# Eight-layer kernel on one core: experts of the second layer a round later on their own bank, ranking behind their weighing; statistics of the seventh layer first in the round

## The reference, cut to what matters

```python
def _L0_ffn_ref(x, W_qkv, b_qkv, W_gate, b_gate, W_experts, b_experts):
    ...
    attn = jax.nn.softmax(attn, axis=-1)
    attn_out = jnp.einsum('bhqk,bkhd->bqhd', attn, v).reshape(B, S, D)
    gate = jax.nn.softmax(x @ W_gate + b_gate, axis=-1)
    top_g, top_i = jax.lax.top_k(gate, TOP_K)
    combine = jnp.sum(jax.nn.one_hot(top_i, E, dtype=x.dtype) * top_g[..., None], axis=2)
    expert_out = jnp.einsum('bsd,edf->bsef', x, W_experts) + b_experts
    moe_out = jnp.einsum('bsef,bse->bsf', expert_out, combine)
    return attn_out + moe_out
```

## Time and profile before

| | us |
|---|---|
| median of 3 runs | 3958.63 (3945.28 to 3960.69) |
| the profiled execution | 3959.01 |
| its span in the profile | 3956.3 |

### The profile page before, as it was taken

The page is one execution under the profiler, slowest core; times in us unless marked ns, Lnnn a source line. Parts: engine busy times, 40 slices in busy tenths (PEclk is TensorE's granted clock), DMA queues, the critical chain, the costliest instruction groups (busy, mean ns, idle before and its releaser), DMA issues.

```text
span 3956.3 us, 106820 instructions
## 1 busy us (share of the span) xinstructions
PE 3214.9 (81%) x39458; PEld 2495.8 (63%) x39458; DVE 2607.1 (66%) x7302; ACT 1752.1 (44%) x4103; POOL 1160.3 (29%) x1193
## 2 busy tenths in 40 slices
PE   6999978888886999976689957766287999999955
PEld 5888854555553666656689945555286777777744
DVE  5677746777775787874454458888423666666679
ACT  4766744555553444432233312222043665665611
POOL 2222223333332333326520024443801223222211
PEclk9999988999997777867799977786599999999966
DMA  3000010000001000011147731110163000000000
GB/s 96 8 9 8 8 24 8 7 7 7 7 7 72 18 17 17 18 15 38 36 168 254 252 111 34 35 32 9 52 217 109 14 11 12 12 11 13 7 17 25
DMA packets 165933, 180.23 MB, mean 46 GB/s; under 512 B 45824, under 2 KB 142848, under 8 KB 165120
## 3 DMA queue, kind: packets, MB, share of 16 engines
q1 hardware_dynamic: 139728, 139.20, 10.8%
q0 software_dynamic: 25600, 28.64, 2.6%
q10 hardware_dynamic: 432, 10.19, 0.6%
HBM read 65.58 MB, written 33.03 MB: 25 GB/s over the span
## 4 chain that ended last, share of the span: by engine, by line
PE 37%; issue 24%; DVE 18%; POOL 9%; DMA 5%; ACT 2%; SPq 2%; another core or an unknown queue 2%; DVEq 0%; POOLq 0%; ACTq 0%
PE ps L965 31%; PE ps L1179 4%; DMA scr_y<-acc 3%; POOL probs L943 3%; DVE mx L1934 2%; POOL arena_a L931 2%; POOL route L937 1%; POOL rstd L920 1%; POOL scr L906 1%; DVE probs L1936 1%; PE ps L1016 1%; DVE den L1947 1%; DVE xn L1844 1%; DVE mx L1923 1%
## 5 line engine op out<-in xcount | busy, mean ns | idle before, releaser
L943 POOL TENSOR_TENSOR probs<-probs,den 128x1024 f32<-128x1024 f32 x128 | 243.2, 1901 | 768.6 <-DVE den L1949 768.6
L965 PE MATMUL ps<-small,xcT 128*64 128x64 f32 (+6 forms) x2976 | 409.6, 355 | 56.1 <-DVE oT L2042 19.7
L1590 ACT ACTIVATE pT<-ps 128x512 f32<-128x512 f32 (+1 forms) x576 | 305.0, 572 | 206.7 <-PE ps L1179 203.9
L965 PE MATMUL ps<-small,oT 128*64 128x128 f32 (+1 forms) x2304 | 326.0, 292 | 28.4 <-ACT oT L1598 16.9
L1179 PE MATMUL ps<-small,probs 128*128 128x128 f32 x2176 | 323.9, 293 | 8.2 <-ACT pT L1590 4.7
L965 PEld LDWEIGHTS ps<-small,oT 128*64 128x64 f32 (+1 forms) x2304 | 279.8, 152 | 75.1 <-ACT oT L1598 24.4
L1598 ACT ACTIVATE oT<-ps 64x512 f32<-64x512 f32 x512 | 288.9, 588 | 78.5 <-PE ps L965 75.5
L1179 PEld LDWEIGHTS ps<-small,probs 128*128 128x128 f32 x2176 | 257.1, 149 | 101.6 <-issue 40.5
L920 POOL TENSOR_TENSOR rstd<-veps,neghalf 128x2 f32<-128x2 f32 (+1 forms) x192 | 147.6, 769 | 576.8 <-DVE veps L1836 382.6
L965 PE MATMUL ps<-arena_b,qT 64*64 64x64 f32 (+3 forms) x10056 | 282.7, 232 | 29.9 <-DVE probs L1920 24.6
L931 POOL DMA_DIRECT2D arena_a<-kT x416 | 216.7, 527 | 279.8 <-ACT kT L1531 263.1
(11 more groups left out here) (291 smaller groups left out, 7454.8 us busy)
## 6 DMA issues: line engine op xcount, KB each, us to landing
wbuf<-parts SPq DMA_DIRECT2D x70, 704.0 KB, 3.5
wbuf<-parts_b SPq DMA_DIRECT2D x39, 512.0 KB, 3.0
scr_y<-acc SPq DMA_DIRECT2D x109, 128.0 KB, 3.4
xcT<-in_ctxT SPq DMA_DIRECT2D x96, 128.0 KB
arena_a<-kT SPq DMA_DIRECT2D x608, 8.0 KB
xcT<-scr SPq DMA_DIRECT2D x70, 128.0 KB, 2.2
arena_a<-kT POOLq DMA_DIRECT2D x416, 8.0 KB
xn<-scr SPq DMA_DIRECT2D x39, 128.0 KB, 2.2
```

The costliest lines, as they stand in the source:

```text
L943: pool.tensor_tensor(pr, pr, rv[:, t, 0:nh].unsqueeze(2).to_broadcast([P, nh, S]), ALU.mult).then_inc(s_probs.sem, 1)
L965: return nc.tensor.matmul(o, lhsT, rhs, start=start, stop=stop, skip_group_check=True)
L1590: nc.scalar.activation(pT[:, t, 4 * j:4 * j + n, :].rearrange("p c t -> p (c t)"), bank(b, n * P), ACT.Copy).then_inc(drained[b], 1)
```

## The change

In `l0f`, C, E and Y lose their `+`: the experts of a group are multiplied, weighed and summed in the round after the one in which it is projected and ranked. They get a ring of their own, `mid_ring`, with bank 5 alone; F, G, QK and V keep bank 4 alone. H moves from before E0.0 to behind R, L from before H to behind E0.0, C from before P1 to before E0.0, Y from before S0 to the round's end. The head sums are taken with 8 products of 256 columns where there were 32 of 64. ACT copies values and sums together into `turned_o`, now `acc` and 512 columns wide (A); PE turns four blocks (R) where it turned two; DVE takes the reciprocal of one column per head (32 where there were 256), multiplies into `o_sb` and adds that to `x_sb`. DVE's update from R now counts on `s_upd`.

In `l3x`, L stands first in the round where it stood behind K3, and M behind K0 where it stood behind W1.

```diff
--- before.py
+++ after.py
@@ -106,15 +106,17 @@
...
         self.front = []
+        self.mid = []
         self.body = []
...
                 continue
-            (self.front if lag == 1 else self.body).extend([item] * uses.get(item[0], 1))
+            part = self.front if lag == 1 else self.mid if item[0] in ("C", "E", "Y") else self.body
+            part.extend([item] * uses.get(item[0], 1))

...

-        return (self.front if item in self.front else self.body).index(item)
+        return (self.front if item in self.front else self.mid if item in self.mid else self.body).index(item)

...
@@ -136,7 +138,7 @@
...
     l0f = Layer(1, "l0f", stages(
-        "F+ S1 G+ QK+ D1 L++ H+ T0- E0.0+ T1- P0 E0.1+ A- V+ E1.0+ E1.1+ R- C+ P1 M++ Y+ S0+ D0+"),
+        "F+ S1 G+ D1 QK+ T0- C E0.0 L++ T1- P0 E0.1 A- M++ E1.0 V+ P1 E1.1 R- H+ S0+ D0+ Y"),
         {"T": 2}, (6, 7), 16, 8 ** -0.5, False, E_FF0, 2)
...
@@ -147,7 +149,7 @@
...
     l3x = Layer(6, "l3x", stages(
-        "F+ T0- S0 T1- P0 S1 Q2+ N0 Q0+ A0- K2+ Q1+ V0+ A1- P1 K0+ N1 W0- Q3+ K3+ L++ V2+ W1- M++ V3+ K1+ V1+"),
+        "L++ F+ T0- S0 T1- P0 S1 Q2+ N0 Q0+ A0- K2+ Q1+ V0+ A1- P1 K0+ M++ N1 W0- Q3+ K3+ V2+ W1- V3+ K1+ V1+"),
         attention, (6, 7), 16, 64 ** -0.5, True)
...
@@ -234,9 +236,12 @@
...
         bank_base.append(dict(base))
-        layer.front_ring = Ring((4, 5), len(layer.front), dict(base))
+        layer.front_ring = Ring((4,) if layer.mid else (4, 5), len(layer.front), dict(base))
         layer.body_ring = Ring(layer.body_banks, len(layer.body), dict(base))
         rings = [layer.front_ring, layer.body_ring]
+        if layer.mid:
+            layer.mid_ring = Ring((5,), len(layer.mid), dict(base))
+            rings.append(layer.mid_ring)
         if layer.heads:
...
@@ -396,7 +401,7 @@
...
         s_relu = step("s_relu", l3f=1)
-        s_upd = step("s_upd", l1x=2, l3f=1)
+        s_upd = step("s_upd", l0f=1, l1x=2, l3f=1)
         s_rank = step("s_rank", l0f=1)
...
@@ -486,7 +491,7 @@
...
         scaled2 = oT[:, 1, :, :].rearrange("p (t e) d -> p t e d", t=2)
-        turned_o = o_sb[:, :, :].rearrange("p t d -> p (t d)")
+        turned_o = acc[:, :, :, :].rearrange("p a t d -> p (a t d)")

...
@@ -994,12 +999,12 @@
...
             def front(layer, item, g):
-                ring = layer.front_ring
+                ring = layer.mid_ring if item in layer.mid else layer.front_ring
                 u = layer.use(item)
...
                 cT = xcT[:, g.par, GT:2 * GT]
-                if u == 1:
+                if u == 1 and ring is layer.front_ring:
                     wait_drained(ring, g, 0)
...
@@ -1108,12 +1113,10 @@
...
                        probabilities, start=a == 0, stop=a == 1)
-                for t, hb, a, j in itertools.product(range(TPG), range(2), range(2), range(4)):
+                for a, j in itertools.product(range(2), range(4)):
                     rows = slice(32 * j, 32 * (j + 1))
-                    at = t * P + hb * S
-                    probabilities = pT[:, t, 2 * j + a, hb * S:(hb + 1) * S]
-                    last = mm(bank(b)[rows, GT + at:GT + at + S], head_ones[:, 16 * a:16 * a + 32],
-                              probabilities, start=a == 0, stop=a == 1)
+                    last = mm(bank(b)[rows, GT:2 * GT].rearrange("p (t n) -> p t n", n=P), head_ones[:, 16 * a:16 * a + 32],
+                              pT[:, :, 2 * j + a, :], start=a == 0, stop=a == 1)
                 last.then_inc(filled[b], 1)
...
@@ -1121,7 +1124,7 @@
...
                     return
-                if item in layer.front:
+                if item in layer.front or item in layer.mid:
                     front(layer, item, g)
...
@@ -1184,8 +1187,8 @@
...
                     b = take(ring, g, u)
-                    for t in range(TPG):
-                        last = nc.tensor.transpose(bank(b)[:, t * P:(t + 1) * P], turned_o[:, t * P:(t + 1) * P], ident)
+                    for n in range(2 * TPG):
+                        last = nc.tensor.transpose(bank(b)[:, n * P:(n + 1) * P], turned_o[:, n * P:(n + 1) * P], ident)
                     last.then_inc(filled[b], 1)
...
@@ -1562,8 +1565,11 @@
...
                     last.then_inc(drained[b], 1)
+                elif kind == "A" and layer is L0F:
+                    b = wait_filled(ring, g, u)
+                    nc.scalar.activation(turned_o, bank(b), ACT.Copy).then_inc(drained[b], 1)
                 elif kind == "C":
-                    b = wait_filled(fr, g, u)
+                    b = wait_filled(layer.mid_ring, g, u)
                     nc.scalar.activation(combT[0:8, g.par, :], bank(b, GT)[0:8, :], ACT.Copy).then_inc(drained[b], 1)
...
@@ -2003,17 +2009,21 @@
...
                     softmax(layer, g, item[1])
-                elif kind == "A" and layer is L0F:
+                elif kind == "R":
                     b = wait_filled(ring, g, u)
-                    inverse = acc[:, 0, :, :].rearrange("p t d -> p (t d)")
-                    dve.reciprocal(inverse, bank(b)[:, GT:2 * GT]).then_inc(s_rv.sem, 1)
+                    sums = bank(b)[:, GT:2 * GT].rearrange("p (t h e) -> p t h e", h=16, e=8)[:, :, :, 0]
+                    dve.reciprocal(rv, sums).then_inc(s_rv.sem, 1)
                     dve.wait_ge(s_rv.sem, s_rv.after(g, 0))
-                    dve.tensor_tensor(turned_o, bank(b, GT), inverse, ALU.mult).then_inc(drained[b], 1)
-                elif kind in ("R", "Y"):
-                    own = ring if kind == "R" else fr
-                    b = wait_filled(own, g, u)
-                    if kind == "R":
-                        wait_drained(fr, g, layer.use(("Y", 0)))
+                    dve.tensor_tensor(o_sb[:, :, :].rearrange("p t (h e) -> p t h e", e=8),
+                                      bank(b, GT).rearrange("p (t h e) -> p t h e", h=16, e=8),
+                                      rv.unsqueeze(3).to_broadcast([P, TPG, 16, 8]), ALU.mult).then_inc(drained[b], 1)
+                    wait_drained(ring, g, u)
+                    wait_drained(layer.mid_ring, g, layer.use(("Y", 0)))
+                    xs = x_sb[:, bass.ds(g.tile(0), TPG), :]
+                    dve.scalar_tensor_tensor(out=xs, in0=o_sb[:, :, :], scalar=tgate[:, layer.n:layer.n + 1], in1=xs,
+                                             op0=ALU.mult, op1=ALU.add).then_inc(s_upd.sem, 1)
+                elif kind == "Y":
+                    b = wait_filled(layer.mid_ring, g, u)
                     xs = x_sb[:, bass.ds(g.tile(0), TPG), :]
...
@@ -2037,13 +2047,13 @@
...
                     t, j = item[1:]
-                    b = wait_filled(fr, g, u)
+                    b = wait_filled(layer.mid_ring, g, u)
                     share = comb[:, g.par, t, 4 * j:4 * j + 4].unsqueeze(2).to_broadcast([P, 4, D])
...
                     if j == 1:
-                        wait_drained(fr, g, layer.use(("E", t, 0)))
-                        wait_drained(fr, g, u)
+                        wait_drained(layer.mid_ring, g, layer.use(("E", t, 0)))
+                        wait_drained(layer.mid_ring, g, u)
                         dve.tensor_tensor(scaled[:, t, :, :], scaled[:, t, :, :], scaled2[:, t, :, :],
...
```

## The result

The changed kernel takes 4042.8 us (median of 4 runs, 4031.6 to 4061.7), the kernel before beside it 3959.7: ratio 1.0215, 95% interval 1.0186 to 1.0245. It is 83 us slower, where 3910 us was predicted. The profiled execution has a span of 4029.8 us, 73.5 more than before's 3956.3.

A forecast was written before the change was run, and what follows sets the result against it. No engine is full; one loop through all engines bounds the second layer, and clock drops lengthen its rounds. 3959.0 − 41 (second layer) − 1 (its first and last rounds) − 7 (seventh layer) = 3910 us, range 3878 to 3957.

The forecast's parts named there:

- 3959 − 41 − 1 − 7: Whole kernel: 41 us off the second layer's periods, 1 off its first and last rounds, 7 off the seventh layer.
- The seventh layer's term, −7: Seventh layer: −0.35 us a round × 31 = −11, and +4 once at the fill.
- the attention product's second half: Second layer's head sums, 8 products of 256 columns for 32 of 64: taken as 1.0 us, as before.
- first expert product to the last weighing: Second layer, first expert product to the last one's end: pieces 7.47 us, taken 7.3 for overlap; single bank hidden.
- The division: Second layer, reciprocal of 32 columns instead of 256: about 0.3 us where it was 1.75.
- rival 3: Second layer: wide attention products don't overlap, 3.6 us instead of 1.0, period 20.7, total 3991 us; chance 0.06.
- Cutting it gains nothing by itself: Second layer at the full clock: new loop 18.0 us against the old 18.1.
- What the clock gives back: Second layer: the clock holds, so the period falls from 19.42 to 18.1 us, 41 us less over 31 periods.
- nowhere does it stand still for 2 us of 3.4: Second layer: TensorE's hole is split into about 1.3, 1.4 and 0.2 us, so the clock should hold.
- the 41: Second layer's expected gain: (19.42 − 18.1) × 31 = 41 us less.
- The 0.49 us at the first transposes: Seventh layer: TensorE's wait of 0.49 us a round for a VectorE copy goes.
- the wait at the first value product: Seventh layer: TensorE's 0.53 us wait for a VectorE copy grows by 0.26, to 0.8 us.

The follow-up runs named there:

- e4: Kernel before with the changed order of the seventh layer alone: 3965.2 us, ratio 1.0038.
- e1: Changed kernel with 60 more TensorE instructions (satisfied waits) ahead of the seventh layer, moving its loop to line 76.00: 3965.0 us, ratio 1.0019.
- e7: Changed kernel, without padding, with TensorE's seventh layer written out instead of a loop of two rounds: 3861.7 us, ratio 0.9958.
- e2: Kernel before with 120 extra TensorE instructions (satisfied waits) ahead of the seventh layer, moving its loop to line 78.33: 4003.7 us, ratio 1.0122.
- e3: Changed kernel with the seventh layer's order of the kernel before: 4031.0 us, ratio 1.0200.
- e15: Changed second layer, old seventh layer, no padding, with products nobody reads in the new loop's two TensorE holes: 3861.6 us, ratio 0.9947.
- e14: Kernel before with unread products in the second layer's two TensorE holes and 192 extra waits ahead of the seventh layer: 3845.5 us, ratio 0.9908.
- e10: e4 once more, on another chip (second layer of before, seventh layer's new order): 3975.4 us, ratio 1.0034.
- e11: Kernel before with the seventh layer's statistics, root and gathers first in the round, normalisation at its old place: 3972.8 us, ratio 1.0030.
- e8: e1 with the seventh layer's normalisation (M) back at its old place behind W1: 3859.3 us, ratio 0.9957.
- e18: e16 with the seventh layer of e8: 3826.7 us, ratio 0.9847.
- e16: Kernel before with one unread product of 384 columns in each of the second layer's two holes, no padding: 3841.5 us, ratio 0.9892.
- e12: e8 once more, on another chip: 3967.7 us, ratio 1.0017.
- e5: e1 with GpSimd's seventh-layer gathers issued at M and no longer in L: 3863.8 us, ratio 0.9951.
- e13: e5 once more: 3866.9 us, ratio 0.9963.
- e17: e16 with the seventh layer of e5 (new order, gathers at the normalisation's place): 3834.7 us, ratio 0.9869.

## Why the prediction was wrong, point by point

**What it left out decided the result.** Of the sum 3959 − 41 − 1 − 7 no term speaks of where the code lies. The seventh layer's term, −7, had bounds of −0.7 to +0.3 us a round; +3.7 were measured, 103 us in all. Of these, 16 ((23.14 − 22.58) × 28, e4) come with its new order on this kind of chip, and the rest with the fetches, (26.27 − 23.15) × 28 = 87 us against e1. Neither was among the rivals, which all priced waits and products. The step that failed stands at the sentence on the attention product's second half, which goes "from 32 products of 64 columns to 8 of 256": I priced its time and put its length in instructions at nothing, and I never asked what follows it in the program.

The Trainium skill has the mechanism (Runtime: NRT & Kernel Launch, section "Instruction fetch mechanics"): a sequencer streams its program in blocks of 16 KiB, TensorE's buffer holds 2048 instructions, and a taken branch whose target is outside the current window of two pages must wait for a fetch. The packets of 16 KB, the stop behind the branch and e7's straight code agree. The same section of the Trainium skill says that the buffer is only two blocks. The trace of before speaks against that for TensorE: a loop of 6.6 blocks runs without a packet.

In these runs the loop's start decides. A loop of 1688 or 1699 instructions stayed in the buffer when it started at 77.86, 78.03, 78.96, 75.99 or 76.00 lines from the program's start, and did not at 78.33 and 75.77. A rule that fits all seven is that it may touch 7 lines and not 8, if what stands ahead of the program is 0.14 to 0.23 of a line long; the rule is inferred from these starts, and its limit was not closed in on. The stop's length differs with the start too: 2.5 to 3.1 us at 78.33 (e2), 5.2 to 6.1 at 75.77 (after and e3), where by the same count at most 23 instructions are left of the first fetched line. That this is the reason was not tested.

**Second layer, the terms at the full clock.** The prediction was 18.0 us; e15 has 18.52. One round of the profile after at the full clock, in order of time, answers to the earlier trace rows:

```profile
755.11 1.13 PE L970 MATMUL ps<-xcT,small 128*128 128x256 f32 x4 [1.36 <-DVE route L1878]
...
758.37 1.12 PE L970 MATMUL ps<-small,xcT 128*128 128x512 f32 x2 [1.04 <-ACT meta L1573]
...
759.53 0.69 DVE L2052 TENSOR_TENSOR oT<-ps,comb 128x512 f32<-128x512 f32 x1 [2.60 <-PE ps L970]
...
761.33 1.99 PE L970 MATMUL ps<-pT,arena_b 128*32 128x64 f32 x80
...
765.16 1.13 PE L970 MATMUL ps<-small,xcT 128*128 128x512 f32 x2 [0.17 <-DVE oT L2052]
...
766.33 0.69 DVE L2052 TENSOR_TENSOR oT<-ps,comb 128x512 f32<-128x512 f32 x1 [1.22 <-PE ps L970]
...
767.73 0.35 DVE L2015 RECIPROCAL den<-ps 128x32 f32<-128x32 f32 x1
...
768.98 0.16 DVE L1886 TENSOR_REDUCE route<-route 128x2 f32<-128x16 f32 x1
...
771.30 1.23 DVE L1936 TENSOR_REDUCE mx<-ps 128x16 f32<-128x1024 f32 x1
...
773.33 0.17 DVE L1878 TENSOR_TENSOR route<-ps,small 128x16 f32<-128x16 f32 x1
...
773.56 1.13 PE L970 MATMUL ps<-xcT,small 128*128 128x256 f32 x4 [1.12 <-DVE route L1878]
```

| term | predicted | measured |
|---|---|---|
| query-key product to first expert product | 3.5 | 758.37 − 755.11 = 3.26 |
| first expert product to the last weighing | 7.3 | 766.33 − 758.37 = 7.96 |
| last weighing and addition, to the division | 1.37 | 1.40 |
| division, multiplication, update | 1.26 | 1.25 |
| ranking | 2.41 | 2.32 |
| maximum, update, bias, to the query-key product | 1.43 + 0.52 + 0.22 | 2.26 |
| sum | 18.0 | 18.45 |

The chain and its order were right, with both new waits (1.04 us for the turned weights, 1.36 and 1.12 for the gate bias) and none for GpSimd. The mis-sized term is the second. I had put 7.47 us down to 7.3 for overlap; instead the single bank shows as a wait of 0.17 us before 765.16, the last weighing starts only at the product's end, and each expert product of 512 columns takes 1.12 us where the earlier trace rows had 1.02, for which no run shows the reason. The division was rightly near 0.3 us, and rival 3 did not happen: the attention product takes 1.99 us in its new form. "Cutting it gains nothing by itself" was right, and too mild: the new loop is 0.5 us a round longer in the mean of e15 against e14. And the round shown is the shorter of the two kinds; in e15's long ones, at the same clock of 1.00, VectorE also stands still for 0.25 us before its update and 0.19 us before the maximum, each time behind an operation of its own.

**What the clock gives back.** The prediction reasoned that no hole is deep enough for the clock to fall, so that 1.3 us a round come back. The clock did fall less often (0.96 against 0.91), but rounds of 19.5 and 22.1 us remained. Here is the start of one of 22.05 us, the stretches' columns as in the earlier trace rows:

```profile
903.28 0.61 PE L970 MATMUL ps<-small,xcT 128*128 128x8 f32 x4
905.24 0.80 PE L970 MATMUL ps<-xcT,small 128*128 128x256 f32 x1 [1.35 <-DVE route L1878]
```

```profile
903.00:904.00 1.00, 0.89 (x8) 0.52 (x4) 0.87 (x1) 0.00 (x0) 0.00 (x0) 1.00 0.00 0
904.00:905.00 1.00, 0.00 (x0) 0.00 (x0) 0.91 (x3) 0.00 (x0) 0.00 (x0) 0.75 0.00 0
905.00:906.00 1.00, 0.76 (x2) 0.67 (x3) 0.90 (x5) 0.00 (x0) 0.32 (x1) 0.50 0.00 0
```

The clock falls in the hole of 1.35 us in front of the query-key product. But the same hole of 1.36 us in front of 755.11 left it at 1.00, so the hole alone doesn't decide it, and what does no run here shows. e15 filled both holes and the clock held. So the step "nowhere does it stand still for 2 us of 3.4" took one example as the limit. That the clock is worth 1.3 us a round in the old order was right: e14 got them. Whether transposes count for it less than products, which the prediction weighed, was not settled: the fall that is shown stands behind a hole in which TensorE did nothing at all, and the fillings were products.

**The base of the sum.** The earlier trace rows is one execution. The second layer of before, unchanged, had 19.42, 19.27, 19.04, 19.42 and 19.27 us a round in the profiles of before, e2, e4, e10 and e11, mean 19.28, with the long rounds (19.7 to 21.1 us, where the clock fell) more or less frequent. The new one had 18.90 to 19.21 in ten profiles, mean 19.03. So its gain is 0.25 × 31 = 8 us, from two sets of profiles that overlap. Of the 33 that are missing from the 41, (18.52 − 18.1) × 31 = 13 are the loop's length, (19.42 − 19.28) × 31 = 4 the base, and (19.03 − 18.52) × 31 = 16 the clock that still falls.

**Seventh layer.** The 0.49 us at the first transposes went, as predicted, and the wait at the first value product came to 0.59 us in e8 (0.8 was expected). On a chip without stops the order gains 22.58 − 22.03 = 0.55 us a round (e7) instead of 0.35, and 0.6 with e8's place of M. The profiled executions of e18 and e16 are 12 us apart (the medians 15), with 17 in the rounds; the 5 between would be the fill, of which I had 4. On a chip with stops the two of them and what they delay cost 1.2 us and turn the gain into +0.6 us a round. The prediction was drawn from one place of the trace and held where nothing else moved.

## What to carry to other kernels

Count instructions as well as microseconds: a loop that nearly fills TensorE's instruction buffer can be tipped over by any edit ahead of it, and a look at the instruction queue's packets before and after shows it at once. Before an order is rebuilt to keep the clock up, fill the hole with products that nobody reads; here that was worth 1.1% (e16) and took a few lines. And take the base of a sum from several profiles where a stage's rounds are not all alike.

## What the runs showed of the hardware

- A branch back to a line that has left TensorE's buffer costs 2.5 to 6.1 us here (e2, e3, after), and every following pass pays it again; straight code fetches 3.3 lines in 22 us without a visible cost (e7, 22.03 us a round).
- Chips differ. Before takes 3955 to 3962 us on some and 3880 to 3886 on others. e8 and e12 are one kernel, with spans of 3857.5 and 3963.6 us at the same mean clock, 0.876. Of the 106 us between them 34 are the longer rounds of the seventh layer, (23.2 − 22.0) × 28, and 58 arise in the fourth layer, while GpSimd issues 128 scatters: from the first to the last it takes 172 us in e8 and 230 in e12. TensorE's unexplained waits in that stage, 1740 to 1950 us of e8 and 1740 to 2000 us of e12:

```profile
PEld ps L970 <- issue: 3.6, 2, 2.8
```

```profile
PEld ps L970 <- issue: 47.3, 17, 8.9
```

  It isn't TensorE alone: VectorE and ScalarE have 27.3 and 24.7 us of such waits there in e12 and none in e8. In both places the stops come while GpSimd issues indirect transfers; that these cause it is argued from the coincidence and was not shown, since all three runs that moved the gathers (e5, e13, e17) fell on chips without the stops.
- A wait that is satisfied isn't free. The seventh layer's first transposes start 0.49 us behind VectorE's normalisation in before (3031.90 to 3032.39), and 0.50 and 0.49 us behind it with e1's 60 and e2's 120 extra instructions, which are done by then. In e14, with 192, the normalisation starts at 2916.66 and the transposes at 2924.79, some 7.6 us late, and TensorE waits there for nothing that the profile shows. If the instructions alone fill these 19.07 us, one takes 0.10 us, an estimate. Before, then e14:

```profile
3032.39 0.66 PE L1016 MATMUL ps<-small,xn 128*128 128x128 f32 x2 [11.37 <-DVE xn L1844]
```

```profile
2924.79 0.66 PE L1021 MATMUL ps<-small,xn 128*128 128x128 f32 x2 [19.07 <-issue]
```
